# Linear attention over 16 images: the input chunks kept ahead, the order of key and output chunks, and the image loop

## What is computed

```python
def _gn(v, G=32, eps=1e-5):
    g = v.reshape(B_, H_, W_, G, C_ // G)
    m = jnp.mean(g, axis=(1, 2, 4), keepdims=True)
    s = jnp.var(g, axis=(1, 2, 4), keepdims=True)
    return ((g - m) / jnp.sqrt(s + eps)).reshape(v.shape)

def _L0_conv_ref(x, W_qkv, W_out, b_out):
    qkv = jnp.einsum('bhwc,cd->bhwd', x, W_qkv)
    q, k, v = jnp.split(qkv, 3, axis=-1)
    # q, k, v reshaped to (b, channel, pixel)
    k = jax.nn.softmax(k, axis=-1)
    context = jnp.einsum('bdn,ben->bde', k, v)
    out = jnp.einsum('bde,bdn->ben', context, q)
    return jnp.einsum('bhwc,cd->bhwd', out, W_out) + b_out

x = x + _L0_conv_ref(_gn(x), W_qkv, W_out, b_out)
```

## Time and profile before

| | |
|---|---|
| median of 3 runs | 1293.5 us (1293.34 to 1297.21) |
| profiled execution | 1297.79 us, of which the span from first to last instruction is 1295.9 us |
| busy: TensorE matmul | 1229.7 us (95% of the span) |
| busy: TensorE weight load | 1137.6 us (88%) |
| busy: VectorE, ScalarE, GpSimd | 853.2, 835.1, 613.8 us |
| DMA moved | 266.99 MB, mean 206 GB/s |
| mean granted TensorE clock | 0.993 |

### The profile page before, as it was taken

One profiled execution on the slowest core, in us unless ns is written; L12 is line 12 of the kernel. 1 busy time (PEld: TensorE's weight loads), 2 busy tenths in 40 slices (PEclk: granted clock), 3 DMA queues, 4 the chain that ended last, 5 costly groups with the idle time before them and its releaser, 6 DMA issues. The chain is left out here.

```text
span 1295.9 us, 23702 instructions
## 1 busy us (share of the span) xinstructions
PE 1229.7 (95%) x8396; PEld 1137.6 (88%) x8396; DVE 853.2 (66%) x1296; ACT 835.1 (64%) x1139; POOL 613.8 (47%) x284
## 2 busy tenths in 40 slices
PE   3899999999999899999999989999999999999998
PEld 3798989989899798988989889898988979899896
DVE  5875848667585755857758477584857758577461
ACT  5566757677585755857667576665857658576763
POOL 7253544545454354553545435445543645435430
PEclk9899999999999999999999999999999999999999
DMA  8248557485665746657486564856657565573523
GB/s 312 94 147 293 206 173 240 162 293 195 233 214 188 246 164 234 217 188 248 155 282 214 183 218 153 306 201 208 213 182 272 174 233 204 192 254 127 195 98 130
DMA packets 109139, 266.99 MB, mean 206 GB/s; under 512 B 12240, under 2 KB 12240, under 8 KB 109008
## 3 DMA queue, kind: packets, MB, share of 16 engines
q1 hardware_dynamic: 109008, 265.34, 59.7%
HBM read 198.18 MB, written 67.11 MB: 205 GB/s over the span
## 5 line engine op out<-in xcount | busy, mean ns | idle before, releaser
L284 POOL TENSOR_TENSOR xt_lo<-xt_raw,xt_hi 128x1024 fp32r<-128x1024 f32 x128 | 307.1, 2407 | 434.3 <-ACT xt_hi L544 429.4
L290 POOL TENSOR_TENSOR x_lo<-x_raw,x_hi 128x1024 fp32r<-128x1024 f32 x128 | 294.3, 2305 | 200.5 <-ACT x_hi L549 200.4
L739 DVE TENSOR_TENSOR mx<-ps_k,mx 128x512 f32<-128x512 f32 x224 | 153.8, 686 | 191.7 <-ACT e_raw L553 172.0
L544 ACT ACTIVATE xt_hi<-xt_raw 128x1024 fp32r<-128x1024 f32 x128 | 134.3, 1063 | 150.9 <-DMA xt_raw<-in_xt_dram 150.8
L771 DVE TENSOR_TENSOR e_lo<-e_raw,e_hi 128x1024 fp32r<-128x1024 f32 x128 | 209.4, 1641 | 29.1 <-ACT e_raw L562 29.1
L328 PE MATMUL ps_k<-wk_hi,xt_hi 128*128 128x256 f32 x1024 | 213.4, 290 | 4.8 <-DVE wk_lo L725 3.0
L328 PE MATMUL ps_k<-wk_lo,xt_hi 128*128 128x256 f32 x1024 | 206.1, 283 | 0.0
L595 ACT ACTIVATE o_stage<-ps_e,bias 128x512 f32<-128x512 f32 x256 | 165.9, 683 | 61.2 <-PE ps_e L463 61.1
L553 ACT ACTIVATE e_raw<-ps_k 128x512 f32<-128x512 f32 x256 | 141.9, 599 | 65.4 <-PE ps_k L328 63.7
L328 PEld LDWEIGHTS ps_k<-wk_hi,xt_hi 128*128 128x128 f32 x1024 | 166.0, 190 | 17.2 <-issue 7.9
L455 PE MATMUL ps_e<-xt_hi,m_hi 128*128 128x512 f32 x512 | 163.6, 401 | 16.5 <-ACT o_stage L595 15.6
(11 more groups left out here) (81 smaller groups left out, 1890.9 us busy)
## 6 DMA issues: line engine op xcount, KB each, us to landing
xt_raw<-in_xt_dram SPq DMA_DIRECT2D x128, 512.0 KB, 5.1
x_raw<-in_xn_dram SPq DMA_DIRECT2D x128, 512.0 KB, 3.3
out_dram<-o_stage SPq DMA_DIRECT2D x256, 256.0 KB, 4.1
xs<-in_xt_dram SPq DMA_DIRECT2D x240, 256.0 KB, 4.6
w_setup<-in_w_dram SPq DMA_DIRECT2D x2, 256.0 KB, 9.8
wk<-in_w_dram SPq DMA_DIRECT2D x1, 256.0 KB, 9.4
wq_t<-in_w_dram SPq DMA_DIRECT2D x1, 256.0 KB, 9.7
b_col<-in_b_out_dram SPq DMA_DIRECT2D x1, 1.0 KB, 10.2
```

The lines of the kernel that those rows point to most:

```text
L284: nc.gpsimd.tensor_tensor(xt_lo[:, s], xt_raw[:, s], xt_hi[:, s].bitcast(F32), ALU.subtract).then_inc(xt_lo_ready, 1)
L290: nc.gpsimd.tensor_tensor(x_lo[:, s], x_raw[:, s], x_hi[:, s, :, 0:C].bitcast(F32), ALU.subtract).then_inc(x_lo_ready, 1)
L739: nc.vector.tensor_tensor(mx[:], ps_k[:, j % 2, h, :], mx[:], ALU.max).then_inc(max_done, 1)
```

## The change

**Buffers.** Chunks 0, 1 and 2 have two `xt` slots (one more), `e_hi` has three buffers (one fewer). The output chunks are taken in the order 3, 4, 5, 6, 7, 0, 1, 2. The table of ones becomes one broadcast column, and `u_sb` gives its place to `m_lo`.

**Orders.** In TensorE's output stage keys 2 comes behind output 0, outputs 1 and 2 follow each other, and from there keys u + 1 stands behind output u; the stage ends with output 7. In the gather stage `turn_max` and `spread_max` come one and a half gather parts earlier. ScalarE and VectorE finish key chunk 7 in the period before; in return `exps(b, 3)` and `e_low(b, 3)` move into the gather stage, as does the rounding of the third doubled chunk. VectorE computes `dm` and `b_mean` with one two-operand instruction each in place of two. SyncE issues the statistics' loads 4 at a time behind outputs 0, 2 and 3, in place of 2 behind each of six.

**Loop.** `images` calls `period` for all 16 images in a row.

```diff
-DOUBLED = (0, 1)
-EMIT_ORDER = (2, 3, 4, 5, 6, 7, 0, 1)
+DOUBLED = (0, 1, 2)
+EMIT_ORDER = (3, 4, 5, 6, 7, 0, 1, 2)
 X_SLOTS = 4
-E_SLOTS = 4
+E_SLOTS = 3
...
+XS_AFTER = {0: (4, 8), 2: (8, 12), 3: (12, 16)}
...
-            period(0, 0, True, True)
-            with engine.Fori(0, (B - 4) // 4) as i:
-                for k in range(4):
-                    period(i * 4 + (k + 1), 1 - k % 2, True, True)
-            period(B - 3, 1, True, True)
-            period(B - 2, 0, True, False)
-            period(B - 1, 1, False, False)
+            for b in range(B):
+                period(b, b % 2, b < B - 1, b < B - 2)
...
-                    if more2 and u < 6:
-                        for q in range(S_SLOTS + 2 * u, S_SLOTS + 2 * u + 2):
+                    if more2 and u in XS_AFTER:
+                        for q in range(*XS_AFTER[u]):
...
-                gather(b, 0)
-                gather_high(b, 1)
-                turn_max(b, 1)
-                if more:
-                    stats_mean(b + 1)
-                gather_low(b, 1)
-                spread_max(b, 1)
-                if more:
-                    stats_var(b + 1)
+                n, np_ = b + 1, 1 - parity
+                gather_high(b, 0)
+                turn_max(b, 1)
+                if more:
+                    stats_mean(n)
+                gather_low(b, 0)
+                gather_high(b, 1)
+                spread_max(b, 1)
+                if more:
+                    stats_var(n)
+                gather_low(b, 1)
...
+                if more:
+                    keys(n, np_, 2)
                 emit(b, parity, 1)
-                emit(b, parity, 2)
-                for u in range(3, NCH):
+                for u in range(2, NCH):
+                    emit(b, parity, u)
                     if more:
-                        if u == 5:
-                            keys_high(n, np_, 4, 0, TILES)
+                        if u == 3:
                             turn_max(n, 0)
-                            keys_low(n, np_, 4, 0, TILES)
+                        if u < NCH - 1:
+                            keys(n, np_, u + 1)
+                        if u == 3:
                             spread_max(n, 0)
-                        else:
-                            keys(n, np_, u - 1)
-                    emit(b, parity, u)
-                if more:
-                    keys(n, np_, 7)
...
-                for d in range(CB):
-                    last = nc.vector.tensor_scalar(dm[:, :, d], m_blk[:, :, d], m_all[:, d:d + 1], None, ALU.subtract)
-                last.then_inc(dm_ready, 1)
+                nc.vector.tensor_tensor(dm[:], m_blk[:], m_all[:].unsqueeze(1).broadcast_to([P, 2, CB]),
+                                        ALU.subtract).then_inc(dm_ready, 1)
```

More of the change, by code:

```diff
@@ L83, in build @@
         grp = sb("grp", [P, P])
-        neg_half = sb("neg_half", [P, CB])
         mx = sb("mx", [P, 2 * C])
         acc = sb("acc", [P, CB, C])
-        u_sb = sb("u_sb", [P, CB, C])
         m_full = acc
         m_hi = sb("m_hi", [P, CB, C], F32R)
+        with nc.sbuf_tensor("u_sb", [P, CB, C], F32) as u_sb:
+            pass
         m_lo = sb("m_lo", [P, CB, C], F32R)
@@ L306, in period @@
             def period(b, parity, more, more2):
+                n, np_ = b + 1, 1 - parity
                 if more:
-                    for j in DOUBLED:
-                        xt_low(b + 1, 1 - parity, j)
-                x_low(b, 4)
+                    xt_low(n, np_, 0)
+                    xt_low(n, np_, 1)
+                for j in range(HALF, NCH):
+                    x_low(b, j)
+                    if j == HALF and more:
+                        rstd_of(n, np_)
                 if more:
-                    rstd_of(b + 1, 1 - parity)
-                for j in range(5, NCH):
-                    x_low(b, j)
-                if more:
+                    pool.wait_ge(wk_ready, n + 1)
+                    xt_low(n, np_, 2)
                     for j in range(X_SLOTS):
[L317 to L320, removed]
+                        x_low(n, j)
+                    for j in range(3, NCH):
+                        xt_low(n, np_, j)
             images(pool, period)
@@ L483, in _ @@
             for d in range(CB):
-                last = nc.tensor.matmul(ps_e[:, 0, 0:C], ones[:], wq_t[:, d, :], start=(d == 0), stop=(d == CB - 1))
+                last = nc.tensor.matmul(ps_e[:, 0, 0:C], one_col[:].broadcast_to([P, P]), wq_t[:, d, :], start=(d == 0), stop=(d == CB - 1))
             last.then_inc(setup_ps, 1)
@@ L636, in period, with both_out @@
                     wk_high(n, np_)
+                wvo_scaled(b, parity)
+                def both_out(j):
+                    if more:
+                        keys_out(n, j, 0)
+                        keys_out(n, j, 1)
                 wq_scaled(b)
@@ L677, in period @@
                     exps(n, 2)
-                    keys_out(n, 6, 0)
-                    keys_out(n, 6, 1)
-                    exps(n, 3)
+                both_out(7)
                 emit(b, 7)
@@ L797, in mean_bias @@
             def mean_bias(b, parity):
-                for c in range(CB):
-                    last = nc.vector.tensor_scalar(b_mean[:, c:c + 1], b_col[:, c:c + 1],
-                                                   neg_mean[:, parity, c:c + 1], None, ALU.subtract)
-                last.then_inc(b_mean_ready, 1)
+                nc.vector.tensor_tensor(b_mean[:], b_col[:], neg_mean[:, parity, :],
+                                        ALU.subtract).then_inc(b_mean_ready, 1)
             def take_u(b, parity):
@@ L854, in _ @@
                 bn_half(1, q)
-            e_low(0, 0)
             shift(0, 2)
             key_maxes(0, 6)
+            e_low(0, 0)
             shift(0, 3)
-            for j in range(1, HALF):
-                e_low(0, j)
+            key_maxes(0, 7)
+            e_low(0, 1)
             bn_sum(1)
+            e_low(0, 2)
             def period(b, parity, more, more2):
@@ L877, in period @@
                 shift(b, 4)
+                e_low(b, 3)
                 if more:
```

68 lines of the change are left out of this document (31 added, 37 removed).

## The result

The changed kernel takes **1263.41 us** (median of 4 runs, 1262.7 to 1264.09); the kernel before took 1293.97 beside it. The ratio is 0.9759, 95% interval 0.9741 to 0.9777: 30.6 us won. Its profiled execution took 1263.93 us with a span of 1262.2, 33.7 less than the span before. The prediction was 1270, within 1250 to 1284.

A forecast was written before the change was run, and what follows sets the result against it. The prediction took TensorE as the bound, its stalls as what can be won. Output stages -34.6, gather stages +9.5 and startup +0.5 gave -24.6 us: 1273.2 against the profiled execution, 1268.9 against the median, stated as 1270, within 1250 to 1284.

The forecast's parts named there:

- Output stages, -34.6: TensorE's 15 output stages: each falls to 41.5 us without stalls, both loop jumps' gaps included, 34.6 us won.
- The timetable: Step times laid out per engine: no load wait in the output stage, 1.75 us of stall in a gather stage.
- the latest point: Output stage, ScalarE's copies of output 4: they end at 22.4 us after output 0 and are wanted at 23.4.
- Gather stages, +9.5: Gather stages of images 1 to 14: the moved e_low(3) meets GpSimd, 26.4 us each in place of 25.72, 9.5 us lost.
- The 1251 "without the lock": Whole kernel: without the VectorE-GpSimd port lock the gather term would be -15.2 us and the forecast 1251.
- Startup, +0.5: Start of the kernel: third doubled chunk ahead of the first statistics and bn_sum moved, +0.5 us, between 0 and 2.
- the forecast of -24.6: Whole kernel: sum of the output, gather and startup terms, a gain of 24.6 us.
- The loop at 0: All 16 images written out: straight-line code brings no issue gaps of its own, priced at 0 us.
- the rival with 2.9 us a period: Written-out code has an issue gap like 2.9 us once a period, adding 41 us: 1311 us, chance 0.03.
- The one with the gather stage unchanged (1263): Gather stages: the 15.2 us are won in whole or part, 1248 us, or 1263 with the stage unchanged; chance 0.22.
- The queue of loads: Output stages: chunk 4 lands 0.8 us late each time, keeping 12 us of stalls, a third: 1282 us, chance 0.15.
- The late load: Output stages: TensorE stalls once chunk 4 lands over 7.1 us after issue; 1306 us at 9.5 us, chance 0.06.

The follow-up runs named there:

- experiment 1: The kernel before with all 16 images written out in place of its loop, nothing else changed: 1284.31 us, ratio 0.9935.
- Experiments 3 to 5: Three chunks ahead, written out: old TensorE order with statistics as before 1281.99 us, with earlier statistics 1264.36; changed kernel with statistics as before 1263.52.
- experiment 7: The kernel before without its loop, two chunks ahead, only VectorE's statistics placed earlier, SyncE's loads two at a time as before: 1300.37 us.
- experiment 9: The changed kernel with chunk 3's e_low reading its second operand from PSUM in place of SBUF (that rest is then wrong): 1249.06 us.
- experiment 2: The changed kernel with the loop of before (3 turns of 4 images) put back: 1267.06 us.
- experiment 8: The changed kernel with SyncE issuing the stores and four statistics loads ahead of chunk 3's load behind output 0: 1301.03 us.
- experiment 6: The kernel before without its loop, two chunks ahead, old order, with VectorE's earlier statistics and SyncE's loads of them four at a time: 1396.68 us, ratio 1.0767.
- experiment 3: The changed kernel with outputs and keys in the old order on TensorE, ScalarE and VectorE, statistics as before: 1281.99 us.

## Why the prediction was right, point by point

- **Output stages, -34.6.** Measured -35.8 (657.08 to 621.24). The timetable held: chunk 3's rounding ended 7.5 us after the end of output 0 (predicted 7.4), without a wait. The copies of output 4, named as the latest point, ended at 23.1 for 23.6, so with 0.5 us to spare in place of 1.0. That the sum came out so close has some luck in it: in the profiled executions 13.7 of the 35.8 us went with the loop alone (657.08 to 643.42, experiment 1). The stage of 46.59 us at a clock of 0.96, in which there was no jump, has no like in experiment 1 either, and it was in the sum that I took the 34.6 from.
- **But the cause was named only in part.** I put the gain down to the key matmuls that a late load now hides behind. Experiments 3 to 5 show that with three chunks ahead what is left is a load that is late because of SyncE's queue, and that moving VectorE's statistics cures it as well. I had the waits of SyncE for the statistics in one sentence, as harmless in the new order, and did not ask what they did in the old one. In the kernel before, with two chunks ahead, they are only a part. Of the 15.6 us of waits for `o_stage`, 9.1 stand ahead of output 4. The load behind that wait in the earlier trace rows went out at 577.13, 1.0 us after output 2, while SyncE stood for VectorE's statistics only later, from 579 to 584; it was the 7.9 us to its use that were long (the median is 5.1), in a stretch in which the DMA engines were this busy. That this made it slow was not tested:

```profile
578.00:586.00 8.00, 7.08 (x46) 1.00 0.89 333
```

The other 6.5 us stand ahead of outputs 5 and 6, most of them behind a load that SyncE issued some 3 us late, behind statistics. And with two chunks ahead the earlier statistics do not cure it (experiment 7: 42.7 us a stage, 42.9 in experiment 1).

- **Gather stages, +9.5.** Measured -1.1 (360.04 to 358.93): the term that was mis-sized. The mechanism and the times up to `x_low(4)` were right: the `e_low(3)` ran from 7.2 to 10.3 (predicted 7.3 to 10.3), `x_low(4)` ended at 12.4 (12.5). From there `x_low(5)` ended at 16.2 in place of 16.6, and the stall of a stage is 25.61 - 24.63 = 0.98 us, not the 0.9 + 0.45 + 0.4 = 1.75 of the timetable. TensorE waits 0.45 us for `x_low(5)`, and the next two come 0.6 to 0.8 us earlier than laid out, so that next to nothing is left of their stalls. The stages before lost about as much (25.72 on average), in two ways: six of the 14 (25.92 to 26.08 us) through a `dm` of 2.9 to 3.05 us, and five (25.48 to 25.55) with a short `dm` through an `e_low` of 2.8 to 3.0 us. So hardly anything changed. Without `e_low(3)`'s block the term would have been -13.5 (346.56 us, experiment 9).
- **The Trainium skill** ("SBUF — State Buffer", section "SBUF: two separate sides") says that a VectorE instruction with two SBUF inputs is locked out while GpSimd reads SBUF. Experiment 9 agrees, with 3.08 us against 1.21 for the same tile when one operand is in PSUM. The 1251 "without the lock" does not follow from its terms: -15.2 in place of +9.5 takes 24.7 us off 1270, which is 1245. That 1249.06 lies near 1251 is luck. The new `dm` with its two SBUF inputs was held too, as that rule of the Trainium skill has it, but for 0.2 us only (predicted 0.4 at most):

```profile
64.43 0.16 DVE L756 TENSOR_TENSOR dm<-m_blk,m_all 128x4 f32<-128x4 f32 x1
...
595.94 2.39 POOL L283 TENSOR_TENSOR xt_lo<-xt_raw,xt_hi 128x1024 fp32r<-128x1024 f32 x1 [8.72 <-ACT xt_hi L543]
...
598.00 0.36 DVE L756 TENSOR_TENSOR dm<-m_blk,m_all 128x4 f32<-128x4 f32 x1
```

In the first image it takes 0.16 us beside an idle GpSimd, in the steady stages 0.36, to GpSimd's end at 598.33.

- **Startup, +0.5.** The first gather starts 1.9 us later (57.87), within the 0 to 2; the last gather stage took 0.8 us more (26.73 for 25.97).
- **Sum.** -35.8 - 1.1 + 1.9 + 0.8 = -34.2, against -33.7 in the spans; the other 0.5 is spread over combine stages and the end. In the spans the forecast of -24.6 was 9.1 us too small a gain: the gather term makes 10.6 of it and the output stages 1.2, and the first and last gather stage take 2.2 back. Against the medians it is 6.6 us (1270 for 1263.41), because the profiled execution of the kernel before was 3.8 us above its median.
- **The loop at 0.** Written-out code showed no issue gap in any period, so the rival with 2.9 us a period is out. Of the gain, 3.7 us (experiment 2) to 9.2 us (experiment 1) are the loop's. The forecast had the two jumps' gaps inside the output term.
- **The rivals.** The one with the gather stage unchanged (1263) is what happened, for another reason than given; it was reckoned from the slower profiled execution, and from the median of 1293.97 it would have been 1259. The queue of loads did not keep a third of the stalls: at 254 GB/s a stage had no wait. That rival set the 357 GB/s of a burst against the mean of a whole stage; in the changed kernel a burst reached nearly as much, without a wait of TensorE:

```profile
640.00:648.00 8.00, 8.00 (x53) 1.00 1.02 348
```

The late load is real: at chunk 3 it is 0.4 us away (experiment 8), as the timetable's own 9.8 for 10.3 had it, while the rival was worked out for chunk 4 alone, with its 2 us of slack.

What stays open: whether two chunks ahead could do without the third. Keys and outputs in turn were not tried with two chunks. Image 14 of experiment 1 loads no statistics and is short with two:

```profile
1182.66:1224.31 41.65, 41.45 (x259) 1.00 0.51 175
```

But it also moves less (175 GB/s, the others 252 to 263), so it cannot tell the waits in the queue from the amount of data. With the statistics' loads in the queue, none of the three runs with two chunks ahead, all in TensorE's old order, came below 42.6 us a stage on average (42.9, 50.3 and 42.7 in experiments 1, 6 and 7).

## What to carry to other kernels

A wait that stands in the queue of the loads for an engine's side work ties all later loads to that engine: before reordering the engine that stalls, look at what the queue waits for between two loads (loading the statistics in groups of four cost 96 us with two chunks ahead, while the changed kernel has the same groups and no wait in its output stages). When two engines hold each other up, moving one instruction moves the meeting; lay out both engines side by side to the end of the stretch and put the work where the other is idle. And a bound that is removed needs one look at the next place, not only at the gain: whether nothing or 13 us was won hung on the place of one line.

## What the runs showed of the hardware

- The hold between VectorE and GpSimd strikes small instructions as hard as large ones: two `dm` of 2 elements a partition took 4.24 us (0.36 in the first gather stage of the kernel before, where GpSimd is idle), two `wk_low` 3.00 in place of 0.87. It goes both ways and by turns: GpSimd's `x_low` takes 3.20 in place of 2.21 when a VectorE instruction was waiting as it began.
- The cost of the same loop jump differs: 2.90 and 3.06 us in the kernel before, 0.90 and 1.89 with the change around it. What makes the difference was not tried.
- Two waits of 2.3 and 3.8 us in an output stage went with a granted clock of 0.93 over it (experiment 6). Stages with single waits of 0.5 to 1.4 us kept 1.00 (experiment 3), and so did those with up to 2.85 us in experiment 8, where one of 3.4 us went with 0.96. Idle gaps of nearly the same length were followed by either level: 2.90 us by a stage at 0.89, 3.06 by one at 1.00.
